# A gated two-stage transformer block on one core: row tiles of the feed-forward prepared inside the last batch of mixing

## What is computed

```python
x = x + tanh(g_xattn[0]) * wkv(w, u, layernorm(x), ctx)         # "mixing": a decayed scan over 512 positions
x = x + tanh(g_ffn[0])   * bit_ffn(layernorm(x), w1, w2, w3)    # the feed-forward
x = x + tanh(g_xattn[1]) * cross_attention(layernorm(x), ctx)   # int8 fake-quantised projections
x = x + tanh(g_ffn[1])   * bitlinear(rms_norm(x), W)

# bit_ffn:
quant_weight(w) = sign(w) * mean(abs(w))
quant_act(x)    = round(clip(x * 127 / s)) * s / 127            # s: max(abs(x)) of each group of 64
bitlinear(x, w) = quant_act(x) @ quant_weight(w).T
h = silu(bitlinear(x, w1)) * bitlinear(x, w2)
out = bitlinear(h, w3)
```

## Time and profile before

| | |
|---|---|
| median of 3 runs | 986.17 us (983.96 to 986.98) |
| the profiled execution's own time | 984.8 us |
| its span, first to last instruction | 983.1 us |
| PE busy | 819.7 us (83%) |
| DVE busy | 760.2 us (77%) |
| ACT busy | 580.1 us (59%) |
| POOL busy | 484.2 us (49%) |
| mean granted clock of TensorE | 0.935 of full speed |

### The profile page before, as it was taken

One profiled execution on the slowest core, in us unless ns is written; L12 is line 12 of the kernel. 1 busy time (PEld: TensorE's weight loads), 2 busy tenths in 40 slices (PEclk: granted clock), 3 DMA queues, 4 the chain that ended last, 5 costly groups with the idle time before them and its releaser, 6 DMA issues.

```text
span 983.1 us, 15282 instructions
## 1 busy us (share of the span) xinstructions
PE 819.7 (83%) x4423; PEld 358.5 (36%) x4423; DVE 760.2 (77%) x1507; ACT 580.1 (59%) x1025; POOL 484.2 (49%) x559
## 2 busy tenths in 40 slices
PE   1279988846999999999999986799999999974654
PEld 1245544412444444444544443132323232321321
DVE  3959989875899999899999767577777777724884
ACT  2348889843455666565656544466666666665862
POOL 1186556212333444444343344466666666674761
PEclk9859999978999999999999996899999999996795
DMA  8537996731333233333323232221212121000111
GB/s 279 213 91 197 230 214 199 193 89 34 69 61 65 54 63 65 59 59 59 58 53 65 55 80 68 76 75 53 80 52 79 52 77 49 1 1 0 43 64 65
DMA packets 165163, 84.51 MB, mean 86 GB/s; under 512 B 116960, under 2 KB 149872, under 8 KB 165104
## 3 DMA queue, kind: packets, MB, share of 16 engines
q1 hardware_dynamic: 165104, 83.81, 33.6%
HBM read 37.50 MB, written 12.58 MB: 51 GB/s over the span
## 4 chain that ended last, share of the span: by engine, by line
PE 55%; DVE 9%; issue 4%; SPq 4%; ACT 3%; DMA 3%; POOL 1%; ACTq 0%; DVEq 0%; POOLq 0%
PE bank L1044 21%; PE bank L1053 10%; PE bank L1128 5%; PE bank L1099 5%; PE bank L1118 4%; DMA A<-B 3%; PE bank L1244 2%; SPq L413 2%; PE bank L1137 2%; PE bank L1147 2%; PE bank L1071 1%; DVE X L1701 1%; SPq L422 1%; DVE B L1582 1%; PE bank L1107 1%
## 5 line engine op out<-in xcount | busy, mean ns | idle before, releaser
L1044 PE MATMUL bank<-A,B 128*128 128x512 f16 x1024 | 232.8, 381 | 18.6 <-DMA B<-B 14.8
L1574 DVE TENSOR_REDUCE B<-bank 128x1 f32<-128x512 f32 x256 | 167.9, 683 | 72.6 <-PE bank L1099 72.5
L872 ACT ACTIVATE A<-bank 128x512 f32<-128x512 f32 x256 | 143.9, 593 | 105.9 <-PE bank L1118 102.3
L538 POOL TENSOR_TENSOR B<-B 128x512 f16<-128x512 f32 x64 | 75.5, 1179 | 206.8 <-ACT B L758 152.8
L1044 PEld LDWEIGHTS bank<-A,B 128*128 128x128 f16 x1024 | 100.2, 98 | 141.3 <-issue 18.0
L616 POOL TENSOR_TENSOR B<-A 128x512 f32<-128x512 f32 x64 | 79.3, 1272 | 92.9 <-ACT A L872 92.9
L1053 PE MATMUL bank<-A,B 128*128 128x512 f16 x512 | 120.7, 379 | 0.0
L753 ACT ACTIVATE bank<-B 128x512 f32<-128x512 f32 x64 | 38.5, 602 | 124.2 <-DVE B L1478 123.8
L1118 PE MATMUL bank<-A 98*128 98x512 f16 x256 | 94.1, 389 | 19.8 <-ACT A L872 10.9
L1099 PE MATMUL bank<-A 96*128 96x512 f16 x256 | 96.9, 404 | 8.8 <-DMA A<-B 4.2
L616 POOL TENSOR_TENSOR B<-B,A 128x512 f32<-128x512 f32 x64 | 79.1, 1269 | 2.4 <-ACT A L872 2.4
(11 more groups left out here) (232 smaller groups left out, 1495.1 us busy)
## 6 DMA issues: line engine op xcount, KB each, us to landing
B<-in_L_ffn_w_dram SPq DMA_DIRECT2D x48, 256.0 KB, 3.1
A<-k_parts SPq DMA_DIRECT2D x48, 128.0 KB, 2.6
A<-B SPq DMA_DIRECT2D x192, 32.0 KB, 1.9
X<-in_x_dram SPq DMA_DIRECT2D x4, 1024.0 KB, 13.6
B<-in_ctx_dram SPq DMA_DIRECT2D x16, 256.0 KB, 5.4
k_parts<-B SPq DMA_DIRECT2D x16, 256.0 KB, 4.6
v_rows<-B SPq DMA_DIRECT2D x16, 256.0 KB, 2.9
B<-v_rows SPq DMA_DIRECT2D x16, 256.0 KB, 3.2
```

Of the source, the lines that this page charges most:

```text
L538: nc.gpsimd.tensor_tensor(HLb[j][:, 1, :], Db[j % 2], HLb[j][:, 0, :], ALU.subtract).then_inc(lo_done, 1)
L872: nc.scalar.activation(PR[(HG * t + j) % 8], bank[2 + j % 2][:, :], ACT.Exp, scale=SCALE).then_inc(exp_done, 1)
L1044: last = mm(bank[2 * n + q][:, :], XQT[a][:, m, :], wt[:, m % DB, j * 512:j * 512 + 512], start=(m == 0), stop=(m == 2 * DB - 1))
L1574: reduce(NMX[g % 2][:, t, j:j + 1], bank[ROW_BANKS[r % 3]][:, :], AX.X, ALU.max, negate=True).then_inc(row_max, 1)
```

## The change

1. **Preparation of tiles 0 and 1 in the last batch.** On VectorE `prep_stats(0)` stands at the end of step 11, `prep_max(0)`, `prep_quant(0)`, `prep_stats(1)` at the end of step 12, `prep_scaled(0)` at that of step 13, `prep_max(1)` and `prep_quant(1)` at that of step 14. On ScalarE `prep_norm(0)` ends step 12, `prep_round(0)` and `prep_norm(1)` step 13, `prep_hi(0)` step 14. GpSimd and SyncE follow. The layout of B for the feed-forward is rearranged: PXN, PT, PD and PHL now lie on mixing's CTX, XQT on CH[0], both no longer used by then.
2. **Weights matrix by matrix.** Step s takes strips 3s to 3s + 2 of the 48 strips in the order w1, w2, w3. The magnitudes of strips of one matrix are summed in one pass, all ahead of `inverse`; only steps 5 and 10 hold two matrices. The pass writes in place.
3. **First products do not wait for the factors.** TensorE's wait for `ff_scales` is replaced by waits at the places of use. The factors are formed around the last residual, the sum over the partitions stands ahead of the last `y_turn`, and the waits for the stores and transposes with the scaling of bp_all go to `mix_over`, between tiles 0 and 1.

```diff
             def pieces(s):
 
                 up_to(sp, signs, s - 1)
-                up_to(sp, abs_done, 3 * (s - 1))
-                b, k = divmod(s, DB)
-                for n, frm in enumerate((w1_rows[s], w2_rows[s], w3_rows[b][:, k * 512:k * 512 + 512])):
-                    sp.dma_start(wst[k % 2][:, n, :], frm).then_inc(piece_in[k % 2], 16)
+                up_to(sp, abs_done, SUMS[s - 1] if s > 1 else 0)
+                for n, (w, i) in enumerate(strips(s)):
+                    b, k = divmod(i, DB)
+                    frm = (w1_rows[i], w2_rows[i], w3_rows[b][:, k * 512:k * 512 + 512])[w]
+                    sp.dma_start(wst[s % 2][:, n, :], frm).then_inc(piece_in[s % 2], 16)
...
                 turn_weights(s)
+                if s == DB * BATCH - 2:
+                    sp.wait_ge(val_ps, DB * BATCH - DB)
+                    turn_x(0, 0)
...
+            def magnitudes(s):
+                act.wait_ge(signs, s + 1)
+                for n, (w, lo, hi) in enumerate(same_matrix(s)):
+                    up_to(act, abs_done, SUMS[s] + n)
+                    part_ = wst[s % 2][:, lo:hi, :].rearrange("p w d -> p (w d)")
+                    nc.scalar.activation(part_, part_, ACT.Abs, accum_out=absw[:, w, s:s + 1]).then_inc(abs_done, 1)
...
-                magnitude(s, 0)
-                magnitude(s, 1)
+                magnitudes(s)
                 inverse(s)
...
                 nc.scalar.copy(KHL[s % 2][:, 0, :], KF).then_inc(key_hi, 1)
-                magnitude(s, 2)
+                if s == DB * BATCH - 4:
+                    act.wait_ge(vT_ps, DB * BATCH)
+                    prep_norm(0)
+                if s == DB * BATCH - 3:
+                    prep_round(0)
+                    prep_norm(1)
+                if s == DB * BATCH - 2:
+                    prep_hi(0)
...
+            pe.wait_ge(means_in, 1)
+            pe.wait_ge(val_sb, DB * BATCH)
+            mm(bank[7][:, 0:3], ones[:, :], PART[:, 0:3], start=True, stop=True).then_inc(setup_ps, 1)
             y_turn(DB * BATCH - 1)
 
 
-            pe.wait_ge(means_in, 1)
-            mm(bank[7][:, 0:3], ones[:, :], PART[:, 0:3], start=True, stop=True).then_inc(setup_ps, 1)
-            pe.wait_ge(ff_scales, 1)
+            pe.wait_ge(signs, -(-2 * TOK // 3) + 1)
...
                         up_to(pe, t_done, c - 1)
+                        if isinstance(c, int) and c == 0:
+                            pe.wait_ge(mixed, DB * BATCH)
...
                 if s > 0:
                     residual(s - 1)
+                if s == DB * BATCH - 5:
+                    prep_stats(0)
+                if s == DB * BATCH - 4:
+                    prep_max(0)
+                    prep_quant(0)
+                    prep_stats(1)
+                if s == DB * BATCH - 3:
+                    prep_scaled(0)
+                if s == DB * BATCH - 2:
+                    prep_max(1)
+                    prep_quant(1)
+
+            dve.wait_ge(abs_done, SUMS[DB * BATCH])
+            reduce(PART[:, 0:3], absw[:, :, :], AX.X, ALU.add).then_inc(means_in, 1)
             values(DB * BATCH - 1)
             ratio(DB * BATCH - 1)
-            residual(DB * BATCH - 1)
...
+            link(ts(SA, MEAN[:, 0:1], 1.0 / XUP, None, ALU.mult))
+            residual(DB * BATCH - 1)
             link(tt(C3, MEAN[:, 0:1], MEAN[:, 1:2], ALU.mult))
...
-            link(recip(C2, TMPS))
-            link(ts(SA, MEAN[:, 0:1], 1.0 / XUP, None, ALU.mult))
...
+            recip(C2, TMPS).then_inc(ff_scales, 1)
...
             tiles(0, True, False)
+            mix_over()
             tiles(1, False, False)
```

More of the change, by code:

```diff
@@ L150, in flamingo_kernel @@
         GROW = T32[0:DB, 8:10, :].bitcast(F16).rearrange("p n (h s) -> p (n h) s", h=2)
-        JUNK = part(512, F32)
         KF = part(512, F32)
@@ L161, in flamingo_kernel @@
         used[0] = 0
-        PXN, PT, PD = part(512, F32), part(512, F32), part(512, F32)
-        PHL = part(1024, F16, "p (h d) -> p h d", h=2)
-        XQT = [part(1024, F16, "p (n t) -> p n t", t=P) for _ in range(2)]
         SAb = [part(512, F32) for _ in range(2)]
@@ L167, in flamingo_kernel @@
         Db = [part(512, F32) for _ in range(2)]
-        HLb = [part(1024, F16, "p (h d) -> p h d", h=2) for _ in range(FC)]
+        HLb = [part(1024, F16, "p (h d) -> p h d", h=2) for _ in range(2)]
+        assert used[0] == 8192
+        PXN, PT, PD = part(512, F32), part(512, F32), part(512, F32)
+        PHL = part(1024, F16, "p (h d) -> p h d", h=2)
+        assert used[0] == 12288
+        HLb += [part(1024, F16, "p (h d) -> p h d", h=2) for _ in range(2)]
         HT = [part(1024, F16, "p (n t) -> p n t", t=P) for _ in range(FC)]
-        gsm = part(64, F32, "p (n g) -> p n g", g=NG)
+        LX, LI = part(D, F32), part(D, F16)
+        LT = part(D, F16, "p (k t) -> p k t", k=DB)
+        assert used[0] == 20480
+        XQT = [part(1024, F16, "p (n t) -> p n t", t=P) for _ in range(2)]
         at = used[0]
@@ L310, in coming, with strips, same_matrix @@
             return slots
+        def strips(s):
+            return [divmod(3 * s + n, TOK) for n in range(3)]
+        def same_matrix(s):
+            of = [w for w, _ in strips(s)]
+            return [(w, of.index(w), of.index(w) + of.count(w)) for w in sorted(set(of))]
+        SUMS = [sum(len(same_matrix(t)) for t in range(s)) for s in range(TOK + 1)]
         def preceding(b, g):
@@ L424, in _ @@
             sp.wait_ge(ff_scales, 1)
-            turn_x(0, 0)
             for i in range(TOK):
@@ L471, in _ @@
             step.link(nc.gpsimd.memset(half[:, :], -0.5))
+            nc.gpsimd.memset(absw[:, :, :], 0.0)
             step.link(nc.gpsimd.iota(IOTA, pattern=[[1, SEQ]], base=0, channel_multiplier=0,
@@ L502, in normed, with prep, prep_lo @@
                 last_.then_inc(xn_ready, 1)
+            def prep(i):
+                pool.wait_ge(st2, i + 1)
+                step.link(nc.gpsimd.tensor_tensor(rs1[:, 0:1], mv1[:, 0, 1:2], eps[:, 0:1], ALU.add))
+                step.link(nc.gpsimd.tensor_tensor(rs1[:, 0:1], rs1[:, 0:1], half[:, 0:1], ALU.pow))
+                step.link(nc.gpsimd.tensor_tensor(nm1[:, 0:1], mv1[:, 0, 0:1], rs1[:, 0:1], ALU.mult))
+                nc.gpsimd.tensor_tensor(sh1[:, 0:1], held[:, 1:2], nm1[:, 0:1], ALU.subtract).then_inc(rstd2, 1)
+            def prep_lo(i):
+                pool.wait_ge(xhl, i + 1)
+                pool.wait_ge(xhi, i + 1)
+                nc.gpsimd.tensor_tensor(PHL[:, 1, :], PD, PHL[:, 0, :], ALU.subtract).then_inc(xlo, 1)
             pool.wait_ge(small_out_dve, 7)
@@ L1049, in down @@
                 pe.wait_ge(hT_in[j], (i + 1) * 16)
+                if isinstance(i, int) and i == 0 and j == 0:
+                    pe.wait_ge(wT_in, 48 * DB * BATCH)
+                    pe.wait_ge(key_f, DB * BATCH)
                 if j == 0:
```

138 lines of the change are left out of this document (55 added, 83 removed).

## The result

| | before | after |
|---|---|---|
| median of 6 runs each, taken together | 986.2 us (983.96 to 988.69) | 977.82 us (974.0 to 978.72) |
| the profiled execution's own time | 984.8 us | 978.03 us |
| its span | 983.1 us | 976.3 us |
| PE busy | 819.7 us (83%) | 826.5 us (85%) |
| ACT busy | 580.1 us (59%) | 573.4 us (59%) |

The ratio is 0.991 (95% interval 0.9888 to 0.9932): 8.4 us less in the median, 6.8 in the span of the profiled executions. TensorE is busy for 6.8 us more although it computes the same (4423 instructions in both), a first sign that some products ran at a lower clock.

The account below looks back on a forecast made before the run. At the handover from mixing to feed-forward the path ends on latency alone, 17.0 us without a large product; VectorE is nearly full. −17.0 + 6.7 + 0.7 = −9.6 took 984.8 to 975.2, stated as 976.0, range 971.5 to 981.5 us.

Parts of the forecast that it names:

- a, −17.0 for the stretch behind the turn: Handover to feed-forward: the stretch without large products between the last turn of y and the first product goes, −17.0 us.
- I leave the clock where it is: First feed-forward products: the first eight still run at 1.2 GHz; the bound the other way is −1.5 us.
- b, +6.7 for the preparation in VectorE's steps: Mixing steps 11 to 14: preparation ahead of each step's ratio on VectorE delays the last turn, +6.7 us.
- the pauses cost the clock: Rival, value products of steps 13 and 15: TensorE's pauses lower the clock, +1.5 to +2.4 us; 979 with d; chance 0.12.
- c, +0.7 for the weights matrix by matrix: Mixing's two-step loop: one wide magnitude pass ahead of the logarithm, +0.7 us, bounds −1.0 and +1.8.
- d, 0 for bp_all between the tiles: Feed-forward between tiles 0 and 1: bp_all is hidden where TensorE is full, up to +0.7 us if not.
- the wait of VectorE: Sign, step 12: VectorE waits about 2.4 us for ScalarE's normalised row before the first maximum.
- the slow clock of the first products: Sign, start of feed-forward: granted clock near 0.5 in the first 3 us of products.
- the shifts of the three ratios: Sign, VectorE: ratios of steps 12, 13 and 14 come 5.2, 4.8 and 6.7 us later, plus what c added.
- slower: Rival, mixing: the weights' transposes land later and hold up the sign pass; up to 998 us, chance 0.04.
- It does not do what it says: Rival, handover: the first product still waits for the transposed tile or factors; 983 us at 7 us more, chance 0.04.
- Better cover: Rival: step 12's 2.4 us wait is avoided and the clock is still high at the first products; 972 us, chance 0.10.

Follow-up runs that it names:

- wait_back: Changed kernel with TensorE waiting for the factors again ahead of the first product: 980.77 us, ratio 0.994 to the kernel before.
- prep_back: Changed kernel with the preparation of tiles 0 and 1 back behind the last step on all engines, parts 2 and 3 kept: 983.5 us, ratio 0.9971.
- warm15: Changed kernel plus 8 idle products, results unread, in TensorE's pause before the value products of step 15: 974.13 us, ratio 0.9879.
- max1_late: Changed kernel with maximum and multiplication of tile 1 moved from step 14 to behind the last step on VectorE: 974.8 us, ratio 0.9879.
- strips_alone: Kernel before with part 2 alone, weights matrix by matrix: 987.06 us, ratio 1.001.
- strips_back: Changed kernel with part 2 undone, one strip of each matrix per step and three magnitude passes: 977.89 us, ratio 0.9918.
- both_moves: Changed kernel with tile 0's statistics and normed row one step earlier and tile 1's maximum and multiplication behind the last step: 972.34 us, ratio 0.9855.
- norm_early: Changed kernel with statistics and normed row of tile 0 one step earlier: 976.67 us, ratio 0.9907.
- both_warm: both_moves plus 11 idle products around the sums, ahead of the last turn of y: 969.85 us, ratio 0.9834 to the kernel before.

## Why the prediction was right

The forecast of 976.0 us stands against a median of 977.82 and, in a second set of runs, 976.48; faster, with both inside the range. The direction came from part 1 together with part 3, as stated: wait_back and prep_back show that the time rises again without either. How near the number came says less than it seems, since two profiles of one kernel differ by up to 3 us and the sum has one term that was 2 us too small. The terms, one by one:

*a, −17.0 for the stretch behind the turn.* It held. The turn's end and the first product are next to each other in every execution with parts 1 and 3, silu did not wait for the factors (the last of them ended at 223.13, silu started at 223.66), and the distance from the turn to the first hidden row fell from 22.97 to 5.66 us, by 17.3. "I leave the clock where it is" was right as well: the first 16 products took 4.75 us (220.64 to 225.39) against 5.1. prep_back and wait_back show how it divides: 2.6 to 3.0 us are part 3's, the other 14 part 1's.

*b, +6.7 for the preparation in VectorE's steps.* This is the term that was too small. The profiled execution came to step 11 already 1.04 later than before (the ratio of that step at 173.28, against 171.42, less the statistics' 0.82). With that taken off, the ratios of steps 12, 13 and 14 were moved by 4.7, 4.8 and 7.0 us, where 5.24, 4.8 and 6.66 were predicted: VectorE's and ScalarE's order was read rightly, the waits included, though a scaling of 1.27 us instead of 0.6 and a shorter wait in step 12 partly cancel in it. The turn was moved by 8.7, where 6.66 were predicted. Of the difference, 1.67 are the value products of step 15 that took 4.43 us instead of 2.76, and the other 0.4 is what the slow products of step 13 cost in step 14. So in this term the mechanism of the main forecast was wrong, which had left the clock out of it, and its rival happened: "the pauses cost the clock", with pauses of 3.6 and 3.4 us (measured 3.64 and 3.41), +1.5 to +2.4 and a chance of 0.12. warm15 and max1_late show it, and the slow products are in every execution that has the changed kernel's steps 14 and 15. The range held because it had been made to take in this rival. It deserved the larger chance, since the pause of 3.4 us was worked out there, beside a row in which the clock had fallen after 3.2. Its payback ("the first product then starts with a higher clock") was 0.38 us over 16 products.

*c, +0.7 for the weights matrix by matrix.* Its price of a wide pass was right (1.47 us and a read of 0.19; the logarithm came 1.47 behind the start of the pass, where 1.49 was worked out). What it does to the time lies below what the medians can tell, as strips_alone and strips_back show; the 0.6 to 1.0 us from scan 11 to the turn without the preparation are of the predicted size, but rest on single profiles. The first profile of the changed kernel was 1.04 late at step 11, the second was not.

*d, 0 for bp_all between the tiles.* It held: the first hidden row comes 7.57 us earlier than before and the products of tiles 1 and 2 by 7.56; the attention that follows starts at 585.07 against 592.63, 7.56 again. The gain stayed, as said; 0.7 us of it is missing in the span, less than two executions of one kernel differ.

So at the first hidden row −17.3 behind the turn, +8.7 from scan 11 to the turn and +1.0 ahead of it make −7.6, where the sum had −9.6. From 984.8 that would give 977.2; the profiled execution's own time was 978.03.

Of the signs named in advance, the wait of VectorE, the wide passes, the slow clock of the first products and, less the 1.04 us above, the shifts of the three ratios came nearly as said. The first product came at 220.64 and 219.47, within the bounds of 214 and 222 but 2 to 3 us later than the 217.45 worked out. The extra transpose went out at 208.28 and landed 3.0 us later, at 211.3 instead of before 211, still 9 us ahead of the first product.

The rival "slower", later landings, did not happen: 2.4, 2.5 and 5.4 us against 2.4, 2.8 and 5.7. "It does not do what it says" did not, since the first product follows the turn. "Better cover" did not either, but both_moves shows that it was to be had, by placing the groups differently.

**What stays open.** Why the clock falls after some pauses of 2 to 3 us and not after others (below); why VectorE's operations and GpSimd's passes lengthen each other, which no run took apart; and the cost of part 2, for which the bounds here are some tenths of a microsecond to 1 us.

## What to carry to other kernels

Work inserted into a full engine cost its own time here and, where TensorE waited for it, the clock of TensorE's next products: look at the pause that it opens and price the products behind it at both levels. Place it where its engine waits anyway (moving two groups by one step gained 3 us of the path here, 1.7 in the median), and trace the whole loop first, since coming earlier to an engine that was not itself earlier gained nothing. A few idle products in a pause ahead of products on the path took 1.6 to 2.8 us off the path, 2.4 and 2.5 in the medians, whose intervals overlap.

## What the runs showed of the hardware

- The pause that costs the clock is not the same every time. The 12 value products ran in 2.76 us behind every pause of 1.3 to 1.93 us, in all executions, and in 4.34 to 5.30 behind 3.20, 3.41 and 3.64. Between them it went both ways: behind 2.74 us they took 2.76 in norm_early and 4.17 in both_moves, and behind 2.73 and 2.12 in both_warm 4.15 and 4.45. The length of the pause alone does not decide between those; no run here separates what does.
- Slow products cost more than their own stretch. The 12 value products of step 13 took 5.30 us, ahead of a step that was 0.2 to 0.4 us longer than in warm15, where they took 4.45.
- VectorE and GpSimd lengthened some of each other's operations in SBUF. VectorE's scaling (L1433, two inputs in SBUF) took 1.27 and 1.28 us where it started 0.4 us behind a low-part pass of GpSimd, and 0.66 in prep_back, where GpSimd ran only a one-column operation. Two operations of 128x8 took 0.63 and 0.84 instead of 0.17 and ended with GpSimd's pass. The other way round, VectorE's multiplication (L1428) kept its 0.69 where it had started first, and GpSimd's pass beside it took 1.46 to 1.62 us instead of 1.15. The maximum over 128x512 (0.67 to 0.69) and the reciprocal of 128x8 (0.20) were not longer beside such a pass. This is observed, not isolated.
